# Eight up products ahead of the first scores, and half of the first deals issued from ScalarE's queue

## The chip, the cores and the metric
One core of a Trainium2 chip runs the whole kernel in one launch. The metric is device time in microseconds. Of the kernel before, three timed runs are known: 924.87, 925.28 and 926.04 us, median 925.28 us.

## The reference, cut to what matters
x has 4 batches of 512 tokens of 256 numbers. Two layers follow each other, each of the form x = x + s * silu(f): s is an attention, f a feed-forward net, both on the normalised x. The change lies in the second layer:

```
xn = layernorm(x)
Q, K, V = xn @ Wq + bq, xn @ Wk + bk, xn @ Wv + bv       # (rows, 256)
q, k, v = 16 heads of 16, 512 tokens each
attn = softmax(q @ k.T / 4);  s = (attn @ v) @ Wo + bo
D = gelu(float16(xn) @ W0.T + bias0)                      # "up": 1024 wide
f = float16(D) @ W1.T + bias1                             # "down"
```

The kernel treats the four batches one after the other, 512 tokens at a time.

## The kernel before, in words
Each engine has its own program, written out by hand; semaphores order them. For every batch b (0 to 3) the first layer runs, then the second. The profile shows four such rounds, some 205 us apart.

In the second layer TensorE makes the query and key products ("qk", four of 128 x 512) and the values. ScalarE (`high_part`) and VectorE (`low_part`) split each into a high and a low float32r part in `stage`. Heads are only 16 numbers long, so the rows are regrouped through device memory: SyncE issues `spill(b, half)` (six stores to `scratch` per half) and then `deal(b, g)` for each of four head groups g (eight loads of 128 KB: for `par` 0 and 1, for `dup` 0 and 1, one into `Qp` and one into `Kp`). A deal writes 32 partitions; par 0 fills partitions 0 to 63, par 1 fills 64 to 127. Half 0 feeds groups 0 and 1, half 1 feeds groups 2 and 3. SyncE's order is spill 0, deal 0, deal 1, spill 1, deal 2, deal 3, and then `max_rows(g)` (L464), which spreads a group's row maxima into `mrow`. The semaphore `dealt[g]` counts the eight loads of a group.

Meanwhile TensorE runs `up1_job(i)` (L1080), the eight "up" products, each six matmuls of 128x512; ScalarE turns each into `H16` with a Gelu (L799, with `gelu_done`). A product's bank is free again when the Gelu four products back is done. Before the change `UP_FIRST` = 6 of them go ahead; then `scores_ahead(0)` waits for `dealt[0]` and issues scores 0 and 1 (L1094); up product 6 follows, scores 2 and 3, up product 7, scores 4 and 5. From score 6 on (`DOWN_FROM` = 3) nine matmuls of "down" (L1153) follow each pair. Three banks form the ring of scores: score m waits until VectorE has taken the maximum of score m - 3 (`maximum`, L1493). After 28 scores (`LEAD`) the turned scores (`scores_turned`, L1126 and L1131) begin; they wait for `m_loaded[0]`, that is, for the maxima of the first group, turned by `turn_max` (L1109), split by `max_high` (ACT) and `max_low` (DVE), and spread by SyncE. `turn_max(1)` waits for 32 maxima (`negate_max`, L1498).

Of the kernel before, what the change touches and what calls it, by code (L numbers as in the profile page):

```python
# [5 lines left out]
F32 = mybir.dt.float32  # L6
# [30 lines left out]
HD = 16  # L37
# [3 lines left out]
HALF = 4 * HD  # L41
# [1 line left out]
LEAD = 4 * GH + 12  # L43
WIDE_FROM = 4 * NH - LEAD
N_SPILL, N_DEAL = 6, 8
UP_FIRST, DOWN_FROM, DOWN_STEP = 6, 3, 9
RSQRT = 13
S16 = SEQ // 32

# [66 lines left out]
def rope_at(s):  # L116

    g, t = s // TT, s % TT
    if g + 1 >= NKV:
        return []  # L120
    return [5 * (g + 1) + i for i in ((0, 1), (2, 3), (4,), ())[t]]


def build(nc, A, out):
    ctx = ExitStack()
    with ctx:
        def sb(name, shape, dt=F32):
            return ctx.enter_context(nc.sbuf_tensor(name, shape, dt))
# [4 lines left out]
        def sig(name, per):  # L133
            return Signal(sem(name), per)
# [44 lines left out]
        Qp = sb("Qp", [P, NPAIR, SEQ], F32R)  # L179
        Kp = sb("Kp", [P, NPAIR, SEQ], F32R)  # L180
# [69 lines left out]
        scratch = nc.dram_tensor("scratch", (2, 2, 2, 3, HD, GH, SEQ), F32, kind="Internal").ap()  # L250
# [28 lines left out]
        spilled = [sig(f"spilled{j}", N_SPILL * 16) for j in range(2)]  # L279
        dealt = [sig(f"dealt{g}", N_DEAL * 16) for g in range(NG)]  # L280
# [100 lines left out]
        def misc_wait(eng, b, name):  # L381
            eng.wait_ge(misc_full, at[b, name] + 1)
# [25 lines left out]
        block = ctx.enter_context(nc.Block())  # L408


        @block.sync
        def _(sp):
            def load_x(b):
# [7 lines left out]
            def load_wrope(b, r):  # L421

                if r >= 5:
                    sp.wait_ge(cos_done.sem, cos_done.at(b, r - 4))
                elif b:
                    sp.wait_ge(cos_done.sem, cos_done.at(b - 1, 5 * NKV + r - 4))
                sp.dma_start(wrope[:, r % 5], A["wrope"][r].rearrange("(c p) n -> p c n", p=P))\
                    .then_inc(wrope_loaded[r % 5].sem, 16)

            def spill(b, half):  # L430

                for which in range(2):
# [3 lines left out]
                    for par in range(2):  # L436
                        src = stage[half][par * HALF:(par + 1) * HALF, which].bitcast(F32)
                        sp.dma_start(scratch[half, which, par, 0:2].rearrange("k d r s -> (d r) k s"), src)                            .then_inc(spilled[half].sem, 16)
                        if which:
                            sp.dma_start(scratch[half, 1, par, 2].rearrange("d r s -> (d r) s"), src[:, 0, :])                                .then_inc(spilled[half].sem, 16)  # L440

            def deal(b, g):


                half, r0 = g // 2, (g % 2) * 2
                if r0 == 0:
                    sp.wait_ge(spilled[half].sem, spilled[half].at(b, N_SPILL * 16))
                for par in range(2):
                    for dup in range(2):
                        rows = slice(par * HALF + dup * 2 * HD, par * HALF + (dup + 1) * 2 * HD)  # L450
                        for dst, which, first in ((Qp, 0, 0), (Kp, 1, dup)):
                            src = scratch[half, which, par, first:first + 2, :, r0:r0 + 2, :]
                            sp.dma_start(dst[rows, 2 * g:2 * g + 2, :].bitcast(F32),
                                         src.rearrange("k d r s -> (k d) (r s)")).then_inc(dealt[g].sem, 16)

            def max_rows(b, g):

# [10 lines left out]
            def store_values(b):  # L468

                sp.wait_ge(v0_ready.sem, v0_ready.at(b, 1))  # L470
                sp.dma_start(v_rows.rearrange("(t p) n -> p t n", p=P), V0[:, :, :]).then_inc(v0_stored.sem, 16)
# [10 lines left out]
            def store(b, t):  # L482
                sp.wait_ge(x2_ready.sem, x2_ready.at(b, t + 1))
                sp.dma_start(out[b, t * P:(t + 1) * P, :], X[:, b % 2, t, :])\
                    .then_inc(out_stored[b % 2].sem, 16)
# [34 lines left out]
            for b in range(B):  # L520
                for r in range(5, 5 * NKV):
                    load_wrope(b, r)
                    if r == 9:
                        store_values(b)
                    if r == 10:
                        load_windows(b)
                    if b and r == 11:
                        for t in range(TT):
                            store(b - 1, t)
                    if b == 0 and r == 9:  # L530
                        load_piece(5)
                    if b == 0 and r == 13:
                        load_ffn1(0)
                if b == 0:
                    for n in range(1, N_F):
                        load_ffn1(n)
                if b + 1 < B:
                    load_x(b + 1)
                    for r in range(5):
                        load_wrope(b + 1, r)  # L540
                for half in range(2):
                    spill(b, half)
                    deal(b, 2 * half)
                    deal(b, 2 * half + 1)
                for g in range(NG):
                    max_rows(b, g)
            for t in range(TT):
# [92 lines left out]
        def _(act):  # L640
# [119 lines left out]
            for b in range(B):  # L760

                if b == 0:
                    prepare(2)
                    act.wait_ge(w_loaded, 16 * N_W)
                    nc.scalar.activation(bo_bc[:, :], bo_bc[:, :], ACT.Copy, scale=0.5).then_inc(bo_halved, 1)
                for s in range(NKV * TT + 1):
                    if s < NKV * TT:
                        if s % TT == 0:
                            key_windows(b, s // TT)
                        for r in rope_at(s) if s == 0 else ():  # L770
                            swap(b, r)
                        exps(b, s)
                        for r in rope_at(s) if s else ():
                            swap(b, r)
                        if b == 0 and s in TURN_UNITS:
                            for k in range(6):
                                turned_weights(6 * TURN_UNITS.index(s) + k)
                        for kind, i in ffn_at(b, s):
                            if kind == "gate":
                                half_tanh(b, i)  # L780
                    if s == OT_UNIT:
                        turned_outputs(b, 0)
                    if b == 0 and 1 <= s <= 3:
                        prepare(s + 2)
                    if b == 0 and 8 <= s < 8 + 2 * N_F:
                        split_ffn1((s - 8) // 2, s % 2)
                turned_outputs(b, 1)
                for t in range(TT):
                    act.wait_ge(f_ready.sem, f_ready.at(b, t + 1))
                    nc.scalar.activation(TE0[:, t, :], F[:, t, :], ACT.Tanh, scale=0.5)\  # L790
                        .then_inc(te_ready.sem, 1)

                for h in range(2):
                    xnT_half(b, h)
                for j in range(4):
                    high_part(b, j)
                for i in range(HC):
                    misc_wait(act, b, ("dup", i))
                    nc.scalar.activation(H16[:, i, 0:SEQ], misc(b, ("dup", i))[:, :], ACT.Gelu,  # L799
                                         bias=b0_sb[:, i:i + 1]).then_inc(gelu_done.sem, 1)  # L800

                def max_high(g):
                    misc_wait(act, b, ("mt", g))
                    nc.scalar.activation(mr[:, 0, :], misc(b, ("mt", g))[0:4 * GH, 0:P], ACT.Copy)\
                        .then_inc(mrhi_ready.sem, 1)

                def half_tanh1(t):
                    act.wait_ge(e_ready.sem, e_ready.at(b, t + 1))
                    nc.scalar.activation(TE1[:, t, :], e16[:, t, 0:DIM], ACT.Tanh, scale=0.5)\
                        .then_inc(te_ready.sem, 1)  # L810

                nc.scalar.activation(warm[:, :], ones1[:, :], ACT.Exp)
                half_tanh1(0)
                max_high(0)
                for t in range(1, TT - 1):
                    half_tanh1(t)
                act.wait_ge(spilled[1].sem, spilled[1].at(b, N_SPILL * 16))
                for g in range(NG):
                    for i in range(4 * GH):
                        n = 4 * GH * g + i  # L820
                        act.wait_ge(t_full.sem, t_full.at(b, L0T + n + 1))
                        nc.scalar.activation(P1[:, n % 8, :], turned_bank(n)[:, :], ACT.Exp, scale=SCALE1)\  # L822
                            .then_inc(p1_ready.sem, 1)
                        if n == 3:
                            half_tanh1(TT - 1)
                        if i == 5 and g + 1 < NG:
                            max_high(g + 1)
                if b + 1 < B:
                    front(b + 1)
# [789 lines left out]
```

## Time and profile before

| what | us |
|---|---|
| median of 3 timed runs | 925.28 |
| the profiled execution | 921.1 |
| its span, first to last instruction | 919.2 |
| TensorE busy | 793.2 (86%) |
| VectorE busy | 620.4 (67%) |
| ScalarE busy | 466.7 (51%) |

The span is the part of the execution that the trace shows; 1.9 us lie around it. The mean granted clock of TensorE over the span is 0.955 of full speed. All times in the rows below are microseconds from the span's start; the second round (batch 1) is the one that most rows are from.

### The profile page before, as it was taken

What the parts mean: (1) busy time and instruction counts of PE and PEld (TensorE: products, weight loads), DVE (VectorE), ACT (ScalarE), POOL (GpSimd) and SP (SyncE); (2) the same over time, 40 slices, a digit from 0 to 9 for tenths busy, and PEclk for the clock granted to TensorE, in tenths of its full rate; (3) what the DMA queues carried; (4) which work ended last, traced back from release to release, by engine and by line L of the source; (5) the groups of instructions that cost most, each with busy time, mean ns of one, the idle gap of its engine ahead of it and who ended that gap; (6) DMA issues with size and microseconds to landing.
All of it is one profiled execution on the core that took longest, in us unless ns stands there. A gap on an engine that the chain in (4) does not pass through costs nothing.

```text
span 919.2 us, 13147 instructions
## 1 busy us (share of the span) xinstructions
PE 793.2 (86%) x4544; PEld 480.1 (52%) x4544; DVE 620.4 (67%) x1653; ACT 466.7 (51%) x948; POOL 313.8 (34%) x264
## 2 busy tenths in 40 slices
PE   3556497787999999997999999997999999987996
PEld 1334265673533666773533666773533666763533
DVE  3886757763985677673985677764986577753972
ACT  4456355423367667322467676232477676232464
POOL 0582857200200788200201888200201888100201
PEclk9876789899999999998999999999999999998999
DMA  7311001208300311008300311018200310018200
GB/s 238 114 31 36 23 1 47 75 0 214 86 1 13 94 52 31 1 22 215 63 3 19 88 52 30 1 42 214 45 3 25 81 30 1 1 39 213 49 3 23
DMA packets 54001, 53.25 MB, mean 58 GB/s; under 512 B 14512, under 2 KB 43568, under 8 KB 53936
## 3 DMA queue, kind: packets, MB, share of 16 engines
q1 hardware_dynamic: 51488, 49.70, 20.4%
q10 hardware_dynamic: 2128, 1.68, 0.6%
q0 software_dynamic: 320, 1.05, 0.4%
q8 instruction: 36, 0.59, 0.3%
q14 instruction: 29, 0.24, 0.1%
HBM read 39.00 MB, written 13.14 MB: 57 GB/s over the span
## 4 chain that ended last, share of the span: by engine, by line
PE 56%; DVE 11%; issue 9%; ACT 8%; POOL 7%; DMA 4%; SPq 3%; POOLq 0%; DVEq 0%; ACTq 0%
PE bank L882 9%; PE bank L987 6%; PE bank L976 5%; PE bank L916 5%; PE bank L1153 5%; PE bank L1141 5%; PE bank L1094 4%; PE bank L1126 3%; PE bank L1048 3%; DVE mx L1493 3%; POOL region L567 3%; PE bank L926 2%; PE bank L1131 2%; PE bank L1080 2%; PE bank L958 2%
## 5 line engine op out<-in xcount | busy, mean ns | idle before, releaser
L1493 DVE TENSOR_REDUCE mx<-bank 128x1 f32<-128x512 f32 x256 | 162.9, 683 | 78.8 <-PE bank L1094 77.8
L882 PE MATMUL bank<-xnT,wrope 128*128 128x512 f32 x320 | 151.1, 615 | 18.5 <-ACT region L712 10.4
L567 POOL TENSOR_TENSOR region<-region 128x512 f32<-128x512 f32 x80 | 106.2, 1327 | 175.4 <-DVE region L1328 170.7
L822 ACT ACTIVATE region<-bank 128x512 f32<-128x512 f32 x256 | 136.3, 597 | 52.5 <-PE bank L1131 48.9
L729 ACT ACTIVATE region<-region,nb 128x128 f32<-128x128 f32 x256 | 81.6, 390 | 97.9 <-DVE nb L1335 97.7
L600 POOL TENSOR_TENSOR region<-region,bo_bc 128x256 f32<-128x256 f32 x16 | 11.7, 729 | 289.0 <-DVE region L1384 289.0
L882 PEld LDWEIGHTS bank<-xnT,wrope 128*128 128x128 f32 x320 | 59.6, 197 | 81.2 <-issue 72.1
L1094 PE MATMUL bank<-Kp,Qp 64*128 64x512 f32 x256 | 68.1, 450 | 23.9 <-DMA Kp<-scratch 20.1
L563 POOL TENSOR_TENSOR region<-region,sin_sb 128x512 f32<-128x512 f32 x60 | 80.4, 1340 | 24.5 <-ACT region L712 23.9
L916 PE MATMUL bank<-region 128*128 128x128 f32 x512 | 75.8, 294 | 11.3 <-ACT region L724 9.7
L1321 DVE TENSOR_TENSOR region<-bank,cos_sb 128x512 f32<-128x512 f32 x80 | 54.7, 688 | 43.5 <-PE bank L882 43.3
L1126 PE MATMUL bank<-Qp,Kp 64*128 64x512 f32 x256 | 75.0, 463 | 7.3 <-ACT region L822 7.3
L916 PEld LDWEIGHTS bank<-region 128*128 128x128 f32 x512 | 65.0, 199 | 25.5 <-issue 11.9
L1341 DVE COPY region<-bank 128x512 f32<-128x512 f32 x64 | 43.9, 686 | 47.2 <-PE bank L926 47.2
L710 ACT ACTIVATE region<-bank 64x512 f32<-64x512 f32 x80 | 47.5, 594 | 52.6 <-DVE region L1321 43.3
L1141 PE MATMUL bank<-region,V 128*17 128x512 f32 x512 | 67.4, 598 | 2.8 <-ACT region L822 2.8
L1126 PEld LDWEIGHTS bank<-Qp,Kp 64*128 64x128 f32 x256 | 30.3, 183 | 73.4 <-ACT region L822 51.3
L987 PE MATMUL bank<-wpT,H 128*128 128x256 f32 x256 | 58.0, 382 | 0.0
L1094 PEld LDWEIGHTS bank<-Kp,Qp 64*128 64x128 f32 x256 | 31.7, 189 | 47.0 <-DMA Kp<-scratch 22.0
L976 PE MATMUL bank<-xnT_hi,wguT 128*128 128x512 f32 x128 | 49.3, 467 | 6.4 <-DVE th L1346 3.7
L987 PEld LDWEIGHTS bank<-wpT,H 128*128 128x128 f32 x256 | 48.0, 190 | 7.1 <-issue 0.6
L1153 PE MATMUL bank<-w1T,H 128*128 128x256 bf16 x384 | 49.6, 274 | 0.0
(135 smaller groups left out, 1345.3 us busy)
## 6 DMA issues: line engine op xcount, KB each, us to landing
wrope<-in_wrope SPq DMA_DIRECT2D x80, 128.0 KB, 2.1
scratch<-region SPq DMA_DIRECT2D x32, 256.0 KB, 3.8
Qp<-scratch SPq DMA_DIRECT2D x64, 128.0 KB, 3.7
Kp<-scratch SPq DMA_DIRECT2D x64, 128.0 KB, 3.9
X<-in_x SPq DMA_DIRECT2D x4, 512.0 KB, 4.0
scratch<-region SPq DMA_DIRECT2D x16, 128.0 KB, 3.3
out<-X SPq DMA_DIRECT2D x16, 128.0 KB, 2.0
VW<-v_rows SPq DMA_DIRECT2D x16, 102.0 KB, 2.8
```

The costliest lines, as they stand in the source:

```text
L567: nc.gpsimd.tensor_tensor(dst, dst, tiles(sw[:, r % 2, :], i), ALU.add)\
L729: nc.scalar.activation(Sm[:, u % 2, i, :], Sm[:, u % 2, i, :], ACT.Exp, bias=nb0[:, u % 2, i:i + 1], scale=-1.0)\
L822: nc.scalar.activation(P1[:, n % 8, :], turned_bank(n)[:, :], ACT.Exp, scale=SCALE1)\
L882: mm = nc.tensor.matmul(misc(b, name)[:, 0:width], lhs(c), xnT[:, c, :], start=(c == 0), stop=(c == DC - 1))
L916: mm = nc.tensor.matmul(s_bank[u % 2][:, i * P:(i + 1) * P], q, keys, start=True, stop=True)
L976: mm = nc.tensor.matmul(misc(b, name)[:, :], wguT[:, c, col:col + P], part[:, c, :], start=(n == 0), stop=(n == 2 * DC - 1))
L987: mm = nc.tensor.matmul(misc(b, ("proj", t))[:, 0:DIM], H[:, c, t * P:(t + 1) * P], wpT[:, c, :], start=(c == 0), stop=(c == HC - 1))
L1094: nc.tensor.matmul(s_ring[m % 3][:, :], Qp[rows, 2 * g + hp, t * P:(t + 1) * P], Kp[rows, 2 * g + hp, :], start=True, stop=True)\
L1126: nc.tensor.matmul(turned_bank(n)[:, :], Kp[rows, 2 * g + hp, keys], Qp[rows, 2 * g + hp, :], start=True, stop=False)
L1141: mm = nc.tensor.matmul(o_bank[h * SLOT:h * SLOT + DVE1, :], V1[:, k, GH * g + h, :], P1[:, n % 8, :], start=(k == 0), stop=(k == TT - 1))
L1153: mm = nc.tensor.matmul(misc(b, name)[:, 0:DIM], H16[:, n % HC, t * P:(t + 1) * P], w1T[:, n // HC, n % HC, :], start=(n == 0), stop=(n == ...
L1493: nc.vector.tensor_reduce(mx1[:, g % 2, column:column + 1], s_ring[m % 3][:, :], AX.X, ALU.max)\
```

## The change
`deal` takes the engine that issues and the parities as arguments, and waits for the spilled half itself each time. For group 0, SyncE issues the four loads of par 0, and ScalarE the four of par 1, between its Gelus 3 and 4. All other deals stay with SyncE. `UP_FIRST` goes from 6 to 8, so that no up product is left between the scores.

```
-UP_FIRST, DOWN_FROM, DOWN_STEP = 6, 3, 9
+UP_FIRST, DOWN_FROM, DOWN_STEP = 8, 3, 9
+DEAL_GELU = 4
+        def deal(eng, b, g, pars):
+            half, r0 = g // 2, (g % 2) * 2
+            eng.wait_ge(spilled[half].sem, spilled[half].at(b, N_SPILL * 16))
+            for par in pars:
+                for dup in range(2):
+                    rows = slice(par * HALF + dup * 2 * HD, par * HALF + (dup + 1) * 2 * HD)
+                    for dst, which, first in ((Qp, 0, 0), (Kp, 1, dup)):
+                        src = scratch[half, which, par, first:first + 2, :, r0:r0 + 2, :]
+                        eng.dma_start(dst[rows, 2 * g:2 * g + 2, :].bitcast(F32),
+                                      src.rearrange("k d r s -> (k d) (r s)")).then_inc(dealt[g].sem, 16)
...
-                    deal(b, 2 * half)
-                    deal(b, 2 * half + 1)
+                    deal(sp, b, 2 * half, range(1) if half == 0 else range(2))
+                    deal(sp, b, 2 * half + 1, range(2))
...
                 for i in range(HC):
+                    if i == DEAL_GELU:
+                        deal(act, b, 0, range(1, 2))
                     misc_wait(act, b, ("dup", i))
```

## Rows read from the trace of the kernel before

**Rows 1.** The page: busy time, and the granted clock in 40 slices.
```profile
PE 793.2 (86%) x4544; PEld 480.1 (52%) x4544; DVE 620.4 (67%) x1653; ACT 466.7 (51%) x948; POOL 313.8 (34%) x264
PEclk9876789899999999998999999999999999998999
```

**Rows 2.** The chain of waits, batch 1, 414 to 429 (start, length, what).
```profile
414.84 3.17 DMA scratch<-region
...
421.20 3.83 DMA Kp<-scratch
...
425.86 2.67 PE bank L1080 x6
```

**Rows 3.** The line of the scores, L1094: what ended its idle time.
```profile
  DMA Kp<-scratch: 42.1, 8
```

**Rows 4.** Timeline of PE, batch 1 (start, length, line, shapes, count, [idle before, releaser]).
```profile
425.07 0.80 PE L1094 MATMUL bank<-Kp,Qp 64*128 64x512 f32 x2 [5.19 <-DMA Kp<-scratch]
425.80 2.74 PE L1080 MATMUL bank<-region,w0T 128*128 128x512 f16 x6
429.10 1.47 PE L1080 MATMUL bank<-region,w0T 128*128 128x512 f16 x6
431.78 0.50 PE L1094 MATMUL bank<-Kp,Qp 64*128 64x512 f32 x1 [0.56 <-DVE mx L1493]
433.30 0.50 PE L1094 MATMUL bank<-Kp,Qp 64*128 64x512 f32 x2
```

**Rows 5.** Timeline of SyncE's queue, batch 1.
```profile
418.02 0.35 SPq L453 DMA_DIRECT2D Qp<-scratch  x1
421.20 0.42 SPq L453 DMA_DIRECT2D Kp<-scratch  x1
439.59 0.42 SPq L453 DMA_DIRECT2D Kp<-scratch  x1
441.39 2.77 SPq L464 DMA_DIRECT2D xnT_hi<-region  x4
```

**Rows 6.** Timeline of ACT: an issue at the start; Gelus 3, 5, 6 of batch 1.
```profile
2.31 0.48 ACTq L644 DMA_DIRECT2D wv_sb<-in_wv  x1
417.32 0.69 ACT L799 ACTIVATE H<-bank,b_sb 128x512 f16<-128x512 f32 x1 [0.61 <-PE bank L1080]
419.92 0.69 ACT L799 ACTIVATE H<-bank,b_sb 128x512 f16<-128x512 f32 x1 [0.61 <-PE bank L1080]
428.57 0.69 ACT L799 ACTIVATE H<-bank,b_sb 128x512 f16<-128x512 f32 x1 [7.97 <-PE bank L1080]
```

**Rows 7.** Half-microsecond windows: five engines' busy times, PEclk, DMA share, GB/s.
```profile
419.00:419.50 0.50, 0.50 (x5) 0.20 (x2) 0.00 (x0) 0.31 (x1) 0.00 (x0) 1.00 0.80 205
421.00:421.50 0.50, 0.00 (x0) 0.00 (x0) 0.00 (x0) 0.00 (x0) 0.00 (x0) 1.00 1.01 205
430.00:430.50 0.50, 0.50 (x5) 0.07 (x3) 0.49 (x1) 0.00 (x0) 0.00 (x0) 1.00 1.07 410
```

**Rows 8.** Timeline of DVE, batch 1.
```profile
425.90 1.29 DVE L1493 TENSOR_REDUCE mx<-bank 128x1 f32<-128x512 f32 x2 [12.71 <-PE bank L1094]
431.03 2.48 DVE L1493 TENSOR_REDUCE mx<-bank 128x1 f32<-128x512 f32 x4 [0.54 <-PE bank L1094]
433.83 1.29 DVE L1493 TENSOR_REDUCE mx<-bank 128x1 f32<-128x512 f32 x2 [0.31 <-PE bank L1094]
```

**Rows 9.** Windows of TensorE's clock, batches 1 and 0 (columns as in Rows 7).
```profile
422.25:425.05 2.80, 0.00 (x0) 0.00 (x0) 0.00 (x0) 0.00 (x0) 0.00 (x0) 0.50 0.99 211
427.05:429.05 2.00, 2.00 (x6) 0.59 (x4) 0.14 (x1) 0.48 (x1) 0.00 (x0) 0.53 1.01 205
217.50:220.30 2.80, 0.00 (x0) 0.00 (x0) 0.00 (x0) 0.00 (x0) 0.00 (x0) 1.00 1.06 222
222.30:224.30 2.00, 2.00 (x6) 0.59 (x4) 0.16 (x1) 0.45 (x1) 0.00 (x0) 0.54 1.05 209
```

**Rows 10.** Timeline of PE, batch 1: the first turned scores.
```profile
448.25 0.50 PE L1126 MATMUL bank<-Qp,Kp 64*128 64x512 f32 x2
```

More of the change, by code:

```diff
@@ L440, in spill @@
                             sp.dma_start(scratch[half, 1, par, 2].rearrange("d r s -> (d r) s"), src[:, 0, :])                                .then_inc(spilled[half].sem, 16)
[L442 to L454, printed above, removed]
             def max_rows(b, g):
```

## The prediction

> **What bounds the kernel now.** I read the page first: TensorE is busy 86% of the span, no other engine over 67%, and the slices of its granted clock dip once in each of the last rounds, where the second layer begins [rows 1]. So I went to that place in the chain of waits. The reader is to see there that, for some 7 us, the chain leaves the engines: it runs through the landing of the last spill (414.84 + 3.17 = 418.02) and then through the landing of a deal into Kp issued at 421.20 (3.83 us), and returns to TensorE at 425.07 [rows 2]. The line of the scores says how often: its idle time that ends with that deal is 42.1 us in 8 entries, two per batch (matmuls and weight loads of the same wait), so about 5 us per batch [rows 3]; in batch 1 it is 5.19 us [rows 4]. A part of the clock is lost too: up product 6, six matmuls, takes 2.74 us after the wait, up product 7 only 1.47 [rows 4], because the clock is at 0.50 (1.2 of 2.4 GHz) from about 422.2 to 429.0 [rows 9].
>
> **Part 1: eight up products first.** Nothing is removed; two products (12 matmuls) move from behind the scores into the wait. Their pace is that of the Gelus before, which wait for TensorE each time: 419.92 - 417.32 is two products, 1.30 us each [rows 6]. TensorE fell idle 5.19 us before 425.07, at 419.88 [rows 4]; with two more products it is busy to 422.48, say 422.5. What hides them is the wait for the deals; if those landed at once, the scores would start 2.6 us later than they could. Banks: product 7 needs the Gelu of product 3, done at 418.01 [rows 6], long before.
> In the present order score 0 goes at 425.07 and score 7 at 431.78, which is 6.71 us for eight scores [rows 4]. Without products between them, the scores are paced by VectorE: a maximum starts 0.53 us after its score's issue (433.30 to 433.83), and four take 2.48 us, 0.62 each [rows 4, 8]. Score 7 waits for maximum 4: 0.53 + 5 x 0.62 + 0.06 for the handover = 3.7 us. From score 7 on the order is the old one, nine down matmuls and two scores, so a shift at score 7 is passed on. The part alone is worth 6.71 - 3.7 = 3.0 us, or about 2.8 with a slow clock in the first scores (the pair at 425.07 takes 0.80 instead of 0.50) [rows 4].
>
> **Part 2: two queues.** SyncE issues a load each (421.20 - 418.02)/7 = 0.454 us [rows 5]; ScalarE's own issues at the kernel's start take 0.48 [rows 6]. So the eighth load of group 0 is issued at about 418.02 + 3 x 0.48 = 419.5, not 421.20: 1.7 us of issue time goes. But issue is not all: data flow from 419.0 at DMA share 1.01 and 205 GB/s [rows 7], 211 in the longer window [rows 9]. Eight loads are 1.05 MB; at 211 GB/s that is 5.0 us, to 424.0, and the scores start 1.07 us after that. If the rate stays, the queues bring next to nothing. The other bound is the rate at 430, 410 GB/s, where one queue held spills of both partition halves [rows 7]: 2.6 us. Rows nearest to the new deals speak for both (the same loads at 205, and both halves in flight at 410), since now par 0 comes from one queue and par 1 from the other, at the same time. I take 300 GB/s, near the middle: 3.5 us. So group 0 is there at 419.0 + 3.5 + 1.07 = 423.6 (bounds 422.7 and 425.0), which is behind the up products' 422.5 in every case.
> ScalarE pays 4 x 0.48 = 1.9 us. It stands behind Gelu 3, which ends at 418.01, and the spill lands at 418.02 [rows 5, 6], so the added wait costs nothing. Queued behind it are Gelus 4 to 7: Gelu 4 would start at about 419.95 rather than 418.62 (419.92 less 1.30), Gelu 5 at 420.65, Gelu 6 at 421.3, and Gelu 7 on time at 422.5. TensorE needs all eight only at the first down matmul, after score 7 (427): cover of 4 us. The cost is 0, and it would begin to count with a spill landing 4 us later.
> SyncE issues four loads fewer, so spill 1 and deals 2 and 3 go up to 1.9 us earlier, and `max_rows(0)` is issued no earlier than behind them: the last of deals 3 is issued at 439.59 and ends at 440.0, max_rows at 441.39 [rows 5]. After: 440.0 - 1.9 = 438.1 at the earliest, a shift of 3.3. The turned scores want it shifted as much as score 7. It ends at 444.16 and they start at 448.25 [rows 5, 10], and within that slack of 4.1 us the small rows still have to land; one landing as long as the deals' 3.83 [rows 2] would leave 0.3. I charge 0 to 0.4 us.
>
> **The sum, batch 1.** Score 7 goes at 423.6 + 3.7 = 427.3 instead of 431.78: 4.5 us. From this comes off the clock. TensorE is idle 422.5 to 423.6 and then works only on eight scores (four pairs of 0.50 us in 3.7 us). In batch 1 the clock fell some 2.3 us after TensorE fell idle (419.88) and stayed low for 6.8; in batch 0 it was still full after 2.8 us of idling, at 220.30, and was low for at most 4, to 224.30 [rows 4, 9]. A microsecond at half clock where TensorE sets the pace costs 0.5 us. I expect one such stretch of 3.4 us (half of the 6.8) in every third batch, 0.6 us on average, and 0.1 for `max_rows`: 3.8 us a batch. All four batches have the same wait [rows 3], and the next batch's front begins only after this layer, so it counts four times: 15.2 us. The profiled execution would be 921.1 - 15.2 = 905.9; the median stands 4.2 above it, so 925.3 - 15.2 = 910.1.
>
> **The rivals.**
> A. Both rates up: 410 GB/s, scores at 422.7, score 7 at 426.4, 5.4 us less 0.3 for max_rows and 0.4 for the clock, 4.7 x 4 = 19: 906. For it: 410 in rows 7. Against: that was stores, of 2 KB each.
> B. The second queue brings no rate: the loads remain at 211 GB/s and the scores start at 425.0. Then part 1 alone counts, 2.8 us, and TensorE idles 2.5 us before them, so the clock falls in nearly each batch and, with sparse scores until 428.7, comes back about 3 us after that: 1.5 us off. 1.3 x 4 = 5: 920. For it: DMA share is already 1.01 [rows 7]. The same comes out if ScalarE's four loads merely share with SyncE's group 1, as both queues would give the last of group 0 after eight loads' worth of data.
> The Trainium skill, "DMA: Bandwidth & Descriptors", section "Issuing engines are not separate DMA queues", says just this: all queues run on the same 16 DMA engines and a second issuer saves sequencer time only. "SBUF — State Buffer", section "Can I just issue two DMAs to hit both halves?", adds that two concurrent ones gained only 6%. By them the time would be B's. The page's port table speaks for less contention between par 0 and par 1, since partitions 0 to 63 reach one half of 16 ports; the 205 GB/s agree with its rate for 32 partitions, the 410 show the halves mixed.
> C. Slower: as B, but the eight bare scores keep the clock at 0.50 for a full 6.8 us beyond score 7 in each batch. That is 3.4 us lost against 2.8 gained, 0.6 x 4 = 2.4: 928. It decides once the low stretch after score 7 exceeds 5.6 us. Against it: today the clock returns within 4 us of the scores' start in both batches [rows 4, 9].
> D. The change does not do what it says: ScalarE reaches its deals late and delays group 0. Bound: Gelu 3 done at 418.01 leaves nothing to be late by, 5% at most, with B's time.
>
> **How the numbers follow.** My forecast has 0.50, A 0.15, B 0.25, D 0.04, C 0.06. The forecast's own range is 907 to 914. The range to hold 8 in 10 runs from 904 (A with no clock loss: 5.1 x 4 = 20.4) to 921, B and a little. A measurement of this kernel can tell 0.2%, 1.9 us: faster is all but C and a part of B and D: 0.91; same 0.04; slower 0.05.
>
> **What would show it.** Right: PE L1080 in one run of 48 matmuls to about 422.5, then scores 0 to 7 with no product between, idle before the first about 1 us and not 5, ended by a deal; score 7 about 3.7 us behind score 0; GB/s over 300 between 419.5 and 422.5; four ACTq issues behind Gelu 3. Wrong: GB/s at 211 there (B), a PEclk of 0.50 beyond score 7 (C, and my 0.6), idle before L1126 that ends with `mrow`'s DMA (my 0.1), or a first down matmul that waits for a Gelu (part 2's cost of 0).

## The result, and the profile after

The kernel after takes 918.11 us (median of 4 runs, 916.98 to 920.59) against 925.35; ratio 0.9925, 95% interval 0.9904 to 0.9946. Timed a second time, in ten runs beside other kernels, it had 918.9 us and 0.9945 (0.9923 to 0.9966). So 5 to 7 us were gained where 15.2 had been forecast. The profiled execution has 917.0 us with a span of 915.2, 4.1 and 4.0 less than before.

The page of the kernel after shows TensorE a little busier. Its clock now dips to 8 tenths at the second layer of every batch (slices 10, 19, 28 and 37); before, it did so only at those of batches 1 and 3 (slices 19 and 37) [rows 1], and not in each as the prediction read it:

```profile
PE 796.7 (87%) x4544; PEld 482.7 (53%) x4544; DVE 619.5 (68%) x1653; ACT 466.4 (51%) x948; POOL 314.0 (34%) x264
PEclk9877789998999999998999999998999999998999
```

The line of the scores (now L1095) says what became of the wait, to be read against [rows 3]: half of it is filled.

```profile
  DMA Kp<-scratch: 20.7, 8
```

Batch 1 in the chain of waits, answering to [rows 2]. The chain now goes through ScalarE's queue, whose last load lands 6.08 us after its issue, where SyncE's had taken 3.83: what the earlier issue won, the landing took back.

```profile
417.77 0.44 ACTq L421
...
418.24 6.08 DMA Kp<-scratch
...
424.37 0.54 PE bank L1095 x2
```

Timeline of PE, batch 1, for [rows 4]: the eight up products in one run, an idle time of 3.01 us, eight scores, and then, unlike before, nine down matmuls that take 2.10 and 2.02 us where 1.16 is their time at full clock.

```profile
410.83 10.52 PE L1081 MATMUL bank<-region,w0T 128*128 128x512 f16 x48
424.37 0.73 PE L1095 MATMUL bank<-Kp,Qp 64*128 64x512 f32 x3 [3.01 <-DMA Kp<-scratch]
425.64 3.18 PE L1095 MATMUL bank<-Kp,Qp 64*128 64x512 f32 x5 [0.55 <-DVE mx L1494]
428.76 2.10 PE L1154 MATMUL bank<-w1T,H 128*128 128x256 bf16 x9
431.52 2.02 PE L1154 MATMUL bank<-w1T,H 128*128 128x256 bf16 x9
433.90 1.16 PE L1154 MATMUL bank<-w1T,H 128*128 128x256 bf16 x9
```

The two queues in batch 1, for [rows 5, 6]: the fourth load of each is issued by 418.7, and the Gelus behind ScalarE's wait.

```profile
416.90 0.35 SPq L421 DMA_DIRECT2D Qp<-scratch  x1
418.22 0.42 SPq L421 DMA_DIRECT2D Kp<-scratch  x1
```

```profile
418.24 0.45 ACTq L421 DMA_DIRECT2D Kp<-scratch  x1
418.73 2.06 ACT L800 ACTIVATE H<-bank,b_sb 128x512 f16<-128x512 f32 x3 [1.83 <-issue]
421.39 0.69 ACT L800 ACTIVATE H<-bank,b_sb 128x512 f16<-128x512 f32 x1 [0.61 <-PE bank L1081]
```

Windows of batch 1, for [rows 7, 9] (busy times of the five engines, then PEclk, DMA share, GB/s): the DMA engines are full (1.05) at 259 GB/s, and the clock is at 0.50 (1.2 GHz) from 426.6 to 433.3, that is, from the middle of the scores until 4.5 us beyond the start of the first down matmul.

```profile
421.40:424.30 2.90, 0.00 (x0) 0.00 (x0) 0.00 (x0) 2.17 (x3) 0.00 (x0) 1.00 1.05 259
426.60:429.60 3.00, 2.99 (x9) 1.46 (x9) 3.00 (x6) 0.00 (x0) 0.00 (x0) 0.50 1.02 367
429.60:433.30 3.70, 3.70 (x17) 2.08 (x15) 1.46 (x3) 0.00 (x0) 0.00 (x0) 0.50 0.40 132
```

Four marks in every batch of both kernels, in us. "Load" runs from the first issue of deal 0 to the first score, "bare" from there to the first down matmul, "turn" from there to the first turned score (L1126 before, L1127 after), and "low" is the time at half clock nearby.

| kernel | load, batches 0 to 3 | bare | turn | low |
|---|---|---|---|---|
| before | 7.03 7.05 7.09 7.52 | 6.94 to 7.44 | 16.03 to 16.04 | 3.4 6.8 3.4 6.8 |
| after | 6.66 7.47 6.83 7.23 | 4.39 to 4.40 | 18.02 to 18.47 | 6.8 in all |

From the first deal to the first turned score this is 30.3 us before and 29.6 after, on average: 0.7 us a batch, 2.8 of the 4.0 by which the spans differ. Most of the rest, 1.5 us, lies between the first turned score of batch 2 and the first deal of batch 3 (176.96 us before, 175.48 after), where nothing was changed; in the other batches that stretch differs by 0.1. Two executions cannot tell whether the change has a part in it.

### The profile page after: what moved, and what is told of

Same layout as the page of the kernel before. It is cut to its first block, busy times and chain, and to the rows that moved or that the text cites. A ratio compares the mean times of both kernels' runs of the same rounds, so it can differ in the third digit from the quotient of the medians.

```text
span 915.2 us, 13147 instructions
## 1 busy us (share of the span) xinstructions
PE 796.7 (87%) x4544; PEld 482.7 (53%) x4544; DVE 619.5 (68%) x1653; ACT 466.4 (51%) x948; POOL 314.0 (34%) x264
## 3 DMA queue, kind: packets, MB, share of 16 engines
q1 hardware_dynamic: 50720, 47.60, 19.4%
q0 software_dynamic: 320, 1.05, 0.4%
## 4 chain that ended last, share of the span: by engine, by line
PE 59%; DVE 12%; issue 9%; ACT 8%; POOL 7%; DMA 4%; ACTq 0%; SPq 0%; POOLq 0%; DVEq 0%
PE bank L883 9%; PE bank L988 6%; PE bank L1154 6%; PE bank L977 5%; PE bank L917 5%; PE bank L1142 5%; PE bank L1095 4%; PE bank L1049 3%; PE bank L1127 3%; DVE mx L1494 3%; POOL region L566 3%; DMA Kp<-scratch 2%; PE bank L927 2%; PE bank L1081 2%; PE bank L1132 2%
## 5 line engine op out<-in xcount | busy, mean ns | idle before, releaser
L1095 PE MATMUL bank<-Kp,Qp 64*128 64x512 f32 x256 | 74.2, 463 | 13.8 <-DMA Kp<-scratch 9.4
L1127 PE MATMUL bank<-Qp,Kp 64*128 64x512 f32 x256 | 75.3, 464 | 7.3 <-ACT region L823 7.3
L1127 PEld LDWEIGHTS bank<-Qp,Kp 64*128 64x128 f32 x256 | 30.4, 183 | 73.4 <-ACT region L823 52.2
L1154 PE MATMUL bank<-w1T,H 128*128 128x256 bf16 x384 | 56.8, 300 | 0.0
L1095 PEld LDWEIGHTS bank<-Kp,Qp 64*128 64x128 f32 x256 | 34.3, 193 | 38.2 <-DVE mx L1494 17.9
```

The costliest lines, as they stand in the source:

```text
L1095: nc.tensor.matmul(s_ring[m % 3][:, :], Qp[rows, 2 * g + hp, t * P:(t + 1) * P], Kp[rows, 2 * g + hp, :], start=True, stop=True)\
L1127: nc.tensor.matmul(turned_bank(n)[:, :], Kp[rows, 2 * g + hp, keys], Qp[rows, 2 * g + hp, :], start=True, stop=False)
L1154: mm = nc.tensor.matmul(misc(b, name)[:, 0:DIM], H16[:, n % HC, t * P:(t + 1) * P], w1T[:, n // HC, n % HC, :], start=(n == 0), stop=(n == ...
```

## The experiments

Ratios are to the kernel before, timed beside each.

**1. Each part alone.** The first takes ScalarE's deals back, the second sets the up products back to six.

```
-                    deal(sp, b, 2 * half, range(1) if half == 0 else range(2))
+                    deal(sp, b, 2 * half, range(2))
...
-                    if i == DEAL_GELU:
-                        deal(act, b, 0, range(1, 2))
```
```
-UP_FIRST, DOWN_FROM, DOWN_STEP = 8, 3, 9
+UP_FIRST, DOWN_FROM, DOWN_STEP = 6, 3, 9
```

> Part 1 alone: eight up products first, all deals from SyncE. Landing theory (the loads of group 0 take about 7 us from their first issue whatever the number of issuers): the first score comes 7.0 to 7.5 us behind the first deal, as in the kernel before (7.03 to 7.52) and after (6.66 to 7.47), and the time is that of the kernel after, 917 to 920. Issue theory (the second queue was worth its 1.7 us): first score over 8 us behind the first deal, 923 to 925. Both expect 4.4 us from first score to first down matmul and a clock at 0.50 for 6.8 us in each batch.

> Part 2 alone: half of the first deals from ScalarE, six up products first. Landing theory: first score 6.7 to 7.5 us behind the first deal and the time of the kernel before, 924 to 926. Issue theory: first score at 5.4 to 6 us behind the first deal, four times 1.5 us faster, 919 to 920. A third reading: Gelus 4 and 5 late by 1.3 us cost nothing in either.

> The kernel after once more, beside kernels that change one thing in it. If the second queue is worth nothing, as its part alone says (ratio 1.000), this is within 0.2% of part 1 alone (ratio 0.9954 to the kernel before); if it adds to part 1, 0.9925 stands.

Eight products first, alone: 919.95 us, 0.9954 (0.9937 to 0.9972), load 7.15 to 7.39, mean 7.23. The split alone: 925.8 us, 1.000 (0.9983 to 1.0018), load 6.94 to 8.28. Both together again: 0.9945 (0.9923 to 0.9966). All of the gain that these runs can tell is part 1's; for the second queue alone the interval leaves room for 1.6 us in all. Beside part 1 it brings the first score 0.2 us sooner on average (load 7.05 against 7.23), and the turn is 0.3 us longer (18.2 against 17.9), so that the turned scores begin no sooner. With part 1 alone the low clock was 6.8 us in three batches and 10.2 in batch 0, at least as long as expected.

**2. What holds group 0.** One kernel lets SyncE wait for group 0 before it issues group 1. The other issues all deals from SyncE, as in the first experiment, and sends the loads to either partition half in turn.

```
+                    if half == 0:
+                        sp.wait_ge(dealt[0].sem, dealt[0].at(b, N_DEAL * 16))
                     deal(sp, b, 2 * half + 1, range(2))
```
```
-            for par in pars:
-                for dup in range(2):
+            for dup in range(2):
+                for par in pars:
```

> As the kernel after, but SyncE issues group 1's loads only when group 0 has landed. Competition theory (SyncE's loads of group 1 take engine time from ScalarE's half of group 0): group 0 lands 1 to 1.5 us sooner, first score 5.2 to 6.0 us behind the first deal. Rate theory (the loads of 32 partitions run at 205 to 230 GB/s by themselves): no change, 6.7 to 7.2. In both group 1 and all behind it on SyncE is some 3 us later, which max_rows must pay for: 0 to 2 us per batch, time 912 to 925.

> As part 1 alone (all deals from SyncE), but in every deal the loads go to partitions 0-63 and 64-127 in turn, instead of four and four. If the rate hangs on whether both partition halves are in flight, it rises over 250 GB/s during the deals and the first score comes under 6.4 us behind the first deal, and max_rows is issued up to 3 us sooner. If it hangs on the loads themselves (4 KB rows read from device memory), it stays at 205 to 230 and the first score at 7.0 to 7.5.

Held back: load 6.26 to 6.74, mean 6.6, half a microsecond better and not 1 to 1.5; the turn grew to 18.7 to 19.4, since max_rows is issued 19 us behind the first score and no longer 16, and TensorE now idles 0.3 to 1.1 us before the turned scores; 920.88 us, 0.9960 (0.9937 to 0.9983). By themselves, the loads of group 0 moved 223 to 238 GB/s. In turn: load 6.52 to 7.22, mean 6.9, and 225 to 241 GB/s where part 1 alone has 224 to 228: more, but not over 250. The time, 919.38 us, 0.9946 (0.9925 to 0.9967), is not to be told from the first experiment's. No one of the theories explains the 7 us alone.

**3. Loads to all partitions.** For group 0 alone, from one contiguous stretch of scratch. The edit shown is that of the wide rows, eight loads of 128 x 1 KB; the narrow rows have eight of 32 x 4 KB, the large loads two of 128 x 4 KB.

```
+            if g == 0:
+                rows = scratch[0, 1].rearrange("p k d (t r) s -> (p k d t) (r s)", t=2)
+                for i in range(8):
+                    dst, c = (Qp, Kp)[i % 2], slice(i // 2 * 256, i // 2 * 256 + 256)
+                    eng.dma_start(dst[:, 0:2, :].bitcast(F32).rearrange("p h s -> p (h s)")[:, c],
+                                  rows[0:P, c]).then_inc(dealt[0].sem, 16)
+                return
```

> Part 1 alone, with other loads in group 0: still eight of 128 KB from SyncE, but each to all 128 partitions (1 KB a row) from one contiguous stretch of scratch; the scores of group 0 are then of other data. Partition theory (a load to 32 partitions cannot run faster than 205 to 230 GB/s): over 330 GB/s between 1 and 4 us behind the first issue, issue-bound, first score 5.4 to 5.9 us behind the first deal. Source theory: unchanged, 7.0 to 7.5.

> The same stretch of scratch for group 0, but eight loads of 32 partitions with 4 KB rows, as the real ones have them; the scores of group 0 are of other data. Partition theory: 205 to 240 GB/s and first score 7.0 to 7.5 us behind the first deal, as in part 1 alone. Source theory (the real loads are slow because they read 4 KB of every 8): under 6 us.

> The loads of the kernel with rows over all 128 partitions, but four issued by SyncE and four by ScalarE as in the change; the scores of group 0 are of other data. If in that kernel the issue of one queue took the place of the partition limit (DMA share 0.72 to 0.83 while the loads ran), a second queue now brings what it did not bring with loads of 32 partitions: over 330 GB/s, first score 5.4 to 6.0 us behind the first deal. If something else holds group 0 (its slowest DMA engine, or the landing), it stays at 6.6 to 7.1.

> The same data of group 0 in two loads of 512 KB from SyncE, one into Qp and one into Kp, all 128 partitions with 4 KB rows. Issue is then 0.9 us in all. Partition theory: first score 1.0 + 1.05 MB at 360 to 400 GB/s + 1.1 = 4.7 to 5.0 us behind the first deal. Rival: 6.6 to 7.1.

> Two loads of 512 KB over all partitions for group 0 (the scores of group 0 are of other data), and SyncE issues group 1's loads only when they have landed. Traffic theory (the loads that follow keep the last part of group 0 back, which landed at 7 us though 350 to 390 GB/s ran): first score 4.6 to 5.2 us behind the first deal. Tail theory (a few DMA engines are late by themselves): 6 to 7 us still.

These kernels ran once each (918.24, 921.59, 924.1, 921.86 and 920.82 us in the order above), so only their traces are used. Load, mean of four batches: wide rows 7.2, narrow rows 7.0, wide rows from two queues 8.4, two large wide loads 6.9, and these with group 1 held back 5.2 (4.86 5.29 5.02 5.60). The wide rows missed their 5.4 to 5.9, the two queues both of their ranges, and the two large loads their 4.7 to 5.0: they came out at the rival's 6.6 to 7.1. With group 1 held back they end at the edge of the traffic theory's 4.6 to 5.2. One window each, batch 1, of narrow rows, wide rows, two large loads, and two large loads with group 1 held back:

```profile
424.00:425.00 1.00, 1.00 (x6) 0.42 (x5) 0.00 (x0) 0.43 (x1) 0.00 (x0) 1.00 1.03 238
```
```profile
421.00:422.00 1.00, 1.00 (x7) 0.42 (x5) 0.00 (x0) 0.39 (x2) 0.00 (x0) 1.00 0.77 244
```
```profile
424.00:425.00 1.00, 1.00 (x7) 0.46 (x5) 0.00 (x0) 0.52 (x1) 0.00 (x0) 1.00 0.98 393
```
```profile
423.00:424.00 1.00, 1.00 (x7) 0.44 (x5) 0.00 (x0) 0.69 (x1) 0.00 (x0) 1.00 0.97 397
```

At full engines loads to 32 partitions run at up to 238 GB/s (share 1.03) and large loads to 128 at 393 and 397 (0.98 and 0.97; in the second nothing is issued behind them): the partition theory holds for the rate. The loads differ in size as well, but the wide rows have loads of 128 KB like the narrow ones, and moved 244 GB/s at a share of only 0.77, by estimate 244 / 0.77 = 317 at full engines. Their expected 330 was out of reach: a load of 128 KB issued every 0.46 us makes 285 GB/s at most. For the landing the theory does not hold: the chain of the kernel with two large loads has the second, issued at 421.81, land 6.51 us later, although its bytes and the first one's need under 3 us at that rate. With nothing issued behind it, the same load lands after 4.86:

```profile
421.81 6.51 DMA Kp<-scratch
```
```profile
420.41 4.86 DMA Kp<-scratch
```

That the loads issued behind group 0 put off its last part is shown by the two kernels that differ in nothing else (6.9 and 5.2). The other thing that holds group 0 is the rate of loads to 32 partitions. Taking one away leaves the other (6.9 and 6.6); without both it is 5.2. The last step also goes from eight loads to two, and eight wide loads with group 1 held back were not run. How the engines share their time between a load and its followers was not seen, and why two queues were slower with wide rows is open.

The kernel with two large loads and group 1 held back also shows something of the clock. TensorE idles only 0.4 to 0.8 us before its scores, less than in the forecast, and the eight bare scores follow; the clock is low for 6.8 us in batches 0 and 3 and for 3.4 in batches 1 and 2 all the same. Batch 1:

```profile
425.31 0.73 PE L1101 MATMUL bank<-Kp,Qp 64*128 64x512 f32 x3 [0.77 <-DMA Kp<-scratch]
```

**4. The clock.** Empty matmuls keep TensorE busy in the wait and between the bare scores.

```
+                def fill(n):
+                    for k in range(n):
+                        nc.tensor.matmul(o_bank[:, :], w0T[:, k % 3, 0, 0:P], x16[:, 0, :], start=True, stop=True)
+                fill(10)
                 for m in range(0, LEAD, 2):
...
                     scores_ahead(m)
+                    if m <= 4:
+                        fill(3)
```

> As the kernel after, plus 19 matmuls of 128x512 that compute nothing that is used: ten behind the last up product, three behind each of the first three pairs of scores. Clock theory (the bare stretch costs by the low clock that follows it): the clock is 1.00 from the first score on, first down matmul to first turned score takes 16.0 us as before the change instead of 18.0 to 18.5, 2.1 us a batch, 909 to 911. Rival (the later stretch waits for VectorE or for max_rows anyway): 16.0 is not reached, 915 to 918.

910.95 us, 0.9847 (0.9829 to 0.9865), with 19 matmuls a batch more than the kernel after. No low clock in any batch, and the turn is 16.46, 16.12, 16.06 and 16.04 in batches 0 to 3. The clock theory's 909 to 911 came out: 7.2 us under the kernel after, and 8.0 under its second timing, though more is computed. That much of the kernel after is thereby shown to be the clock's. In batch 3 TensorE idles 1.73 us before the first score, as the deal landed late, and the clock stays up there too, with the gaps between the scores filled. In batch 1 the down matmuls take 1.16 us from the start, and between 424 and 428 the clock is 1.00, where the kernel after had fallen to 0.50 by the end of the scores:

```profile
427.64 1.16 PE L1154 MATMUL bank<-w1T,H 128*128 128x256 bf16 x9
```
```profile
424.00:428.00 4.00, 4.00 (x19) 1.61 (x19) 3.99 (x7) 0.00 (x0) 0.00 (x0) 1.00 1.03 285
```

**5. Useful work in the same place.** First the down matmuls between the bare scores, then also max_rows ahead of group 3's deals, then 12 down matmuls in the wait itself. The last two kernels take ScalarE's deals back, or hold group 1 as in the second experiment.

```
-UP_FIRST, DOWN_FROM, DOWN_STEP = 8, 3, 9
+UP_FIRST, DOWN_FROM, DOWN_STEP = 8, 0, 7
```
```
-                    deal(sp, b, 2 * half + 1, range(2))
+                    if half == 0:
+                        deal(sp, b, 1, range(2))
                 for g in range(NG):
                     max_rows(b, g)
+                    if g == 0:
+                        deal(sp, b, 3, range(2))
```
```
+UP_FIRST, DOWN_AHEAD, DOWN_STEP = 8, 12, 6
...
+                pe.wait_ge(gelu_done.sem, gelu_done.at(b, HC))
+                down(0, DOWN_AHEAD)
                 for m in range(0, LEAD, 2):
...
+                    n = DOWN_AHEAD + DOWN_STEP * (m // 2)
+                    down(n, n + DOWN_STEP)
```

> As the kernel after, but the down matmuls begin behind the first pair of scores, seven a step (DOWN_FROM 0, DOWN_STEP 7): real work in the bare stretch. From the first score to the first turned score 14 steps of 0.43 + 7 x 0.12 = 1.28 us make 17.9 us instead of 22.4 to 22.9. Clock and VectorE theory: 17.9 to 18.5, 4 us a batch, 901 to 904. SyncE theory (max_rows stands behind the deals of groups 2 and 3, its first issue 15.3 to 15.9 us behind the first score): the turned scores begin 20 us behind the first, 2.5 us a batch, 907 to 910.

> As the last, and max_rows of group 0 goes ahead of the deals of group 3 in SyncE's queue. SyncE theory: the turned scores come 18 us behind the first score, 1.5 to 2 us a batch better than the last kernel, 900 to 903. Clock and VectorE theory: as the last kernel within 0.2%.

> As the kernel with down early and max_rows of group 0 ahead of group 3's deals, and now 12 down matmuls stand ahead of the first scores, in the wait for the deals, and six follow each pair. Clock theory: TensorE is idle under 1.2 us at any one time there, the clock stays at 1.00, first score to first turned score takes 19.4 us in every batch (as in the one undisturbed batch of the last kernel) against 20.2 with the empty matmuls: 907 to 909. Rival (the clock falls all the same, as TensorE waits for VectorE in each step): 911 to 914.

> The same with all deals from SyncE, in turn for either partition half. If the second queue is worth nothing, within 0.2% of the last kernel; if it is worth its issue time, 1.2 us a batch slower, 912 to 914.

> The kernel with 12 down matmuls ahead, and group 1's loads held back until group 0 has landed. Held back with no other change, group 0 came 0.5 us sooner (6.6 us behind the first deal against 7.0), which four times is 2 us: 904.5 to 906.5 against 906.9. Rival: group 1 and all that SyncE issues behind it are 3 us later, and max_rows of group 0 comes too late again: 908 to 912.

| kernel | us | ratio (95%) | first score to first turned, batches 0 to 3 | low clock |
|---|---|---|---|---|
| down early | 915.1 | 0.9890 (0.9866 to 0.9914) | 20.94 20.89 19.85 20.90 | 3.4 3.4 0 3.4 |
| and max_rows first | 913.31 | 0.9866 (0.9845 to 0.9886) | 20.96 20.90 21.84 19.40 | 3.4 3.4 6.8 0 |
| and 12 down ahead | 906.92 | 0.9809 (0.9789 to 0.9829) | 19.12 19.09 19.11 19.12 | none |
| the same, all from SyncE | 907.81 | 0.9821 (0.9803 to 0.9838) | 19.11 19.08 19.10 19.10 | none |
| 12 down ahead, two queues, group 1 held | 904.50 | 0.9778 (0.9754 to 0.9803) | 20.15 19.10 19.09 19.09 | none |

The first two missed their 901 to 904 and 900 to 903, and the first its rival's 907 to 910 too: after the idle wait before the scores, which they leave, the clock still fell in three batches of four, and 17.9 was too low a floor. Their own times can't be told apart (the intervals overlap), against the 1.5 to 2 us a batch that max_rows' place was expected to bring. In the one batch of each whose clock stayed up, the way to the turned scores is 19.85 and 19.40; the first idles 0.40 us right before them and the second not at all, so max_rows' place is worth about 0.4 us where the clock holds. The floor is VectorE's: from the first maximum of the fastest kernel to its first turned score, 422.93 to 441.49 in batch 1, VectorE is busy 18.53 of 18.56 us. It takes 13 maxima without a gap and goes on with other work at once:

```profile
422.93 8.11 DVE L1498 TENSOR_REDUCE mx<-bank 128x1 f32<-128x512 f32 x13 [12.02 <-PE bank L1099]
430.95 0.42 DVE L1514 TENSOR_TENSOR region<-bank,b_bc 128x256 f16<-128x256 f32 x1
```

With work in the wait the clock stays up in each batch: 906.92 us beside the 907 to 909 expected. The timeline of PE of the fastest kernel, batch 1, shows the wait filled: 0.78 us idle for the last Gelu, 12 down matmuls, and the scores with no wait for a deal.

```profile
420.98 1.48 PE L1158 MATMUL bank<-w1T,H 128*128 128x256 bf16 x12 [0.78 <-ACT H L804]
422.39 0.50 PE L1099 MATMUL bank<-Kp,Qp 64*128 64x512 f32 x2
```

The second queue again makes no difference (0.9809 and 0.9821). Holding group 1 gives the fastest kernel, 904.5, at the edge of its 904.5 to 906.5: 2.2% under the kernel before, and by the ratios 1.5 to 1.7% under the kernel after. With the hold the scores wait for a deal in no batch; without it they did in two, 1.09 and 0.28 us. In its batch 0 the rival's price shows: 0.98 us idle before the turned scores, which come 20.15 us behind the first and not 19.1, with max_rows issued later. That it is faster than without the hold is not shown, as the intervals overlap.

## Why the prediction was wrong

- **Where the time is, and part 1: right.** The wait for group 0's loads was the place. Score 0 to the first down matmul fell from 7.12 us on average to 4.39, by 2.7; forecast 2.8 to 3.0. Score 7 went 3.67 us behind score 0 in every batch, as the 3.7 worked out. The eight up products took the 10.5 us worked out for them.
- **Part 2: wrong, the term of the rate.** "I take 300 GB/s, near the middle" put the first score 5.6 us behind the first deal. It came after 7.05 on average, as before (7.17). That was the bound of 425.0, rival B's, and the split alone is worth 1.000. The step took the 410 GB/s of the spills as a sign for these loads; alternating halves in one queue did not bring it either. Where over 300 GB/s was to be seen, 249 ran, at a DMA share of 0.89 (418.4 to 421.4, the kernel after being 1.1 us early). With group 1 held back the first score still came only after 6.6: so some 1.0 us of the miss is the rate, and 0.5 the followers, for SyncE's loads of group 1 now stand beside ScalarE's half of group 0, whose last load took 6.08 us to land. Rival B named that sharing; the forecast's time left it out. The loads were to bring 1.5 us a batch and brought 0.1.
- **The cover of ScalarE's issues: right.** Gelus 4 to 6 ran 418.73 to 420.79, Gelu 7 at 421.39 on TensorE's pace, all before the first score.
- **The clock: wrong, mis-sized.** "One such stretch of 3.4 us in every third batch, 0.6 us on average" was 6.8 us in every batch, and the turn grew from 16.03 to 18.2: 2.1 us a batch. Filling the gaps took just this away. It does not follow from the longer wait alone: with two large loads and 0.4 to 0.8 us of idling the clock fell in every batch too, after the sparse scores, which the forecast saw and priced at those 0.6. Rows 1 had a warning that was misread: the page before dips in two second layers of four. The mechanism was rival C's. Counted from score 7, as C counts, the clock stayed low for 5.0, 5.3, 6.0 and 5.3 us, little under the 5.6 beyond which C has the change turn slower, and in batch 2 above it.
- **max_rows: right to leave small.** With the clock held and all else as in the change, the turn is within 0.1 us of that of before in three batches; only in batch 0 does TensorE idle, 0.35 us, before the turned scores.
- The sum by measured terms: 2.7 + 0.1 - 2.1 = 0.7 a batch, 2.8 in all, beside 4.0 in the profiled spans and 5 to 7 by the timed runs; single executions of the kernel before lie between 921.6 and 930.2, and where the rest comes from in those was not seen. The time fell between rival B (920) and the forecast (910.1). That it lies within 904 to 921 is no merit of the forecast's mechanism: the range was drawn to reach rival B. And it came out faster than before only because the clock's loss, 2.1, stayed under part 1's gain, 2.7.
- The Trainium skill's sentence in "DMA: Bandwidth & Descriptors", "Issuing engines are not separate DMA queues", that a second issuer saves sequencer time only, was the one to follow; the trace agrees, with 1.000 for the split alone. The port table of "SBUF — State Buffer" ("Door 1: The DMA port swizzle") gives 32 partitions half of the ports and at most about 218 GB/s, and 128 partitions all of them and 436. The runs agree in kind, with 393 and 397 to 128; to 32 they show 205 to 238, so the figure is a little low here.

## What to carry to other kernels

Before giving loads a second queue, look at the DMA share while they run: at 1.0, as here, an earlier issue only lengthens the landing. When a wait is filled or a stretch is thinned out on TensorE, count the busy time around it too: what is saved in the wait can be lost to a half clock in the dense stretch behind it, and real work moved into the wait and between the scores (here 12 down matmuls ahead and six behind each pair) gave more than the change itself. A load's landing depends on what is issued behind it: here 1.7 us for two large loads, 0.5 for the eight small ones. What a hold of the followers delays behind them has to be counted with it: for the eight small loads the later max_rows took the 0.5 back and more (turn 18.7 to 19.4 against 18.0 to 18.5).

## What the runs showed of the hardware that was not expected

- A load of 512 KB landed 6.51 us after its issue with other loads behind it and 4.86 without them, the data rate being 393 and 397 GB/s; on average over four batches the first score came 6.9 and 5.2 us behind the first issue.
- Loads to 32 partitions filled the DMA engines at 205 to 238 GB/s; the same engines moved 393 to 397 to 128 partitions.
- The clock stayed low 6.8 us in all four batches after an idle time of only 2.0 to 3.0 us followed by eight sparse scores, and fell in all four batches, for 3.4 or 6.8 us, after only 0.4 to 0.8 us of idling before the same scores (two large loads, group 1 held). Ten matmuls in the wait and three behind each of three pairs kept it up.
